# Latent attention: ScalarE copies sums and products out of PSUM, VectorE divides in SBUF in halves, and the marking of choices moves back

## What is computed

```
def attention(x, kv_d_w, q_d_w, k_u_w, v_u_w, q_u_w, rope_k_w, rope_q_w, o_w):
    kv_d, q_d = x @ kv_d_w, x @ q_d_w                     # 512 -> 128
    k, q = ...   # 16 heads of 16 + 16 features, the second 16 rotated (rope)
    v = (kv_d @ v_u_w).reshape(b, s, NH, HD)
    scores = jnp.einsum('bqhd,bkhd->bhqk', q, k) * scale  # causal
    probs = jax.nn.softmax(scores, axis=-1)
    out = jnp.einsum('bhqk,bkhd->bqhd', probs, v).reshape(b, s, H)
    return out @ o_w
h = x + attention(rmsnorm(x, ln1_w), ...)
out = h + moe(rmsnorm(h, ln2_w), ...)     # sigmoid router over 7 experts, the best 2 of each token
```

## Time and profile before

| | |
|---|---|
| time, median of 3 runs | 2374.48 us (2373.86 to 2377.71) |
| profiled execution | 2374.67 us, of it span 2372.9 us |
| TensorE busy | 2136.2 us, 90% of the span |
| VectorE busy | 1362.6 us, 57% |
| ScalarE busy | 805.7 us, 34% |
| GpSimd busy | 669.1 us, 28% |
| granted TensorE clock, mean | 0.96 |
| iterations 0 to 15 of the latent attention | about 1584 to 2041 us; TensorE busy 403.6 of 457 us |

### The profile page before, as it was taken

How to read it: one execution, slowest core, us unless ns; L and a number is a source line. 1 busy time by engine, 2 the same in 40 slices (tenths; PEclk the granted TensorE clock), 3 DMA queues, 4 the chain that set the end, 5 groups by cost and what they waited for, 6 DMA issues and landing times. The chain is left out here.

```text
span 2372.9 us, 31623 instructions
## 1 busy us (share of the span) xinstructions
PE 2136.2 (90%) x10998; PEld 1176.1 (50%) x10999; DVE 1362.6 (57%) x3185; ACT 805.7 (34%) x1333; POOL 669.1 (28%) x945
## 2 busy tenths in 40 slices
PE   9999989989999999879999987588888888889994
PEld 5777748854444444445555543133333333336763
DVE  5866768856222126566777774755656565445443
ACT  5654624420122211334444432523222232123333
POOL 0300014526433321224343443011113131224453
PEclk9999999999999999899999999699999999999997
DMA  7211222270177764363333430200000000065555
GB/s 258 86 36 54 89 104 100 94 292 1 55 235 249 247 190 149 104 130 84 80 88 82 89 68 1 97 3 2 2 19 2 19 28 19 18 184 154 102 98 172
DMA packets 101179, 230.33 MB, mean 97 GB/s; under 512 B 18886, under 2 KB 42626, under 8 KB 93870
## 3 DMA queue, kind: packets, MB, share of 16 engines
q1 hardware_dynamic: 78478, 186.61, 25.5%
q0 software_dynamic: 22560, 41.87, 8.0%
HBM read 169.45 MB, written 63.53 MB: 98 GB/s over the span
## 5 line engine op out<-in xcount | busy, mean ns | idle before, releaser
L2145 DVE CUSTOM_DVE_ANT_0 D_ps<-D_ps,D_mask 128x256 f32<-128x256 f32 (+1 forms) x512 | 186.6, 420 | 60.8 <-PE D_ps L2041 59.9
L1925 ACT ACTIVATE D_probs<-D_ps 128x512 f32<-128x512 f32 (+1 forms) x256 | 125.4, 543 | 178.3 <-PE D_ps L2063 178.2
L1867 POOL TENSOR_SCALAR_AFFINE_SELECT D_probs<-D_probs 128x256 f32<-128x256 f32 x256 | 106.1, 420 | 282.4 <-ACT D_probs L1925 282.3
L3178 DVE TENSOR_REDUCE F_neg_max<-F_ps 128x4 f32<-128x2048 f32 (+1 forms) x64 | 93.9, 1488 | 107.6 <-PE F_ps L3076 101.5
L2928 ACT ACTIVATE F_probs<-F_ps 128x1536 f32<-128x1536 f32 (+1 forms) x48 | 76.4, 1591 | 187.5 <-PE F_ps L3092 187.5
L1400 PE MATMUL C_ps<-C_down_shared,C_hs 128*128 128x512 f32 x256 | 115.4, 600 | 2.4 <-DVE C_hs L1568 2.4
L1388 PE MATMUL C_ps<-C_xT,C_gate_shared 128*128 128x512 f32 x256 | 115.4, 594 | 0.8 <-DMA C_up_shared<-moe_sh_up_dram 0.8
L1388 PE MATMUL C_ps<-C_xT,C_up_shared 128*128 128x512 f32 x256 | 115.1, 592 | 0.0
L2041 PE MATMUL D_ps<-D_k_stack,D_q_stack 96*128 96x256 bf16 (+1 forms) x512 | 93.9, 269 | 15.1 <-DVE D_maxima L2145 12.2
L1237 POOL DMA_INDIRECT expert_sums<-C_y,C_of_slot x32 | 50.3, 1570 | 173.4 <-ACT C_y L1304 111.2
L2809 POOL TENSOR_SCALAR_AFFINE_SELECT F_probs<-F_probs 128x512 f32<-128x512 f32 x64 | 41.1, 654 | 179.9 <-ACT F_probs L2928 179.9
(11 more groups left out here) (578 smaller groups left out, 4943.7 us busy)
## 6 DMA issues: line engine op xcount, KB each, us to landing
C_ring<-moe_experts_dram SPq DMA_DIRECT2D x32, 1536.0 KB, 7.0
qk_parts<-D_parts SPq DMA_DIRECT2D x32, 384.0 KB, 2.6
expert_sums<-A_zeros SPq DMA_DIRECT2D x1, 8192.0 KB
C_ring<-expert_sums SPq DMA_DIRECT2D x5, 1536.0 KB, 13.8
D_q_stack<-qk_parts SPq DMA_DIRECT2D x16, 384.0 KB, 4.7
D_k_stack<-qk_parts SPq DMA_DIRECT2D x16, 384.0 KB, 7.8
B_w<-ctxT_dram SPq DMA_DIRECT2D x1, 4096.0 KB, 16.7
B_c<-ctx_dram SPq DMA_DIRECT2D x4, 1024.0 KB, 7.8
```

Of the source, the lines that this page charges most:

```text
L1867: last = nc.gpsimd.affine_select(now[:, :, 0:P], now[:, :, 0:P], [[0, 2], [1, P]], ALU.is_ge, 0.0, base=0, channel_multiplier=-1)
L1925: nc.scalar.activation(probs[at % 2][:, 2 * pair:2 * pair + 2, 0:w], ps[:, 4 + unit % 3, :].rearrange("p (h q) -> p h q", h=2)[:, :, 0:w], ...
L2145: last = nc.vector.tensor_tensor_reduce(now, now, mask[:, first:256], 1.0, -3e38, ALU.add, ALU.max, maxima[n % 2][:, head, t:t + 1])
L3178: last = nc.vector.tensor_reduce(neg_max[n % 2][:, :, t], ps[:, 0:GROUP, at:at + w], AX_X, ALU.max, negate=True)
```

## The change

ScalarE gets a new step at the head of slot 0, `keep_pv(n)` for the chunk just finished, before the first exponential of the next: it waits for `pv_in_psum`, for the divisions of all chunks before (`oT_ready`), and, from the second batch on, for the output products of the batch before (`out_ready`), and copies bank 5 to `rden` and bank 4 to `oT`. The signal `pv_kept` follows. TensorE's first `times_v` of the next chunk waits for `pv_kept` and no longer for `oT_ready`. VectorE's `divide` waits for `pv_kept` and works in place in SBUF: where the new iteration begins a batch (i % 4 = 0, so also for the last chunk) all 512 columns at slot 0, else 256 columns at slot 0 and 256 at the head of slot 2, where `oT_ready` follows. `mark` of batches 0 to 2 moves from two to four places after "turn_z", to place 3, which is behind the maximum of slot 1; in the last batch it stays where it was.

```diff
--- before.py
+++ after.py
@@ -2727,8 +2727,8 @@
     v_in_psum, v_ready, out_ready, summed = (sem(n) for n in ("v_in_psum", "v_ready", "out_ready", "summed"))
     scores_ready, max_ready, max_turned, m_hi_ready, m_rest_ready, m_mid_ready, m_lo_ready = (sem(n) for n in (
         "scores_ready", "max_ready", "max_turned", "m_hi_ready", "m_rest_ready", "m_mid_ready", "m_lo_ready"))
-    scoresT_ready, exp_ready, cut_ready, probs_read, pv_in_psum, oT_ready = (sem(n) for n in (
-        "scoresT_ready", "exp_ready", "cut_ready", "probs_read", "pv_in_psum", "oT_ready"))
+    scoresT_ready, exp_ready, cut_ready, probs_read, pv_in_psum, pv_kept, oT_ready = (sem(n) for n in (
+        "scoresT_ready", "exp_ready", "cut_ready", "probs_read", "pv_in_psum", "pv_kept", "oT_ready"))
     dve_step = sem("dve_step")
     evicted = {"turn_x": xT_ready, "low": low_ready, "rope": raw_ready, "turn": turned_taken, "nope": nope_ready,
                "values": v_ready, "out": summed, "turn_m": m_rest_ready, "turn_h": h_kept, "logits": zT_ready, "turn_z": e_ready,
@@ -2927,9 +2927,22 @@
                 act.wait_ge(pv_in_psum, n)
             nc.scalar.activation(probs[u][:], ps[:, 0:GROUP, 0:WIDTH[u]], ACT.Exp, scale=1.0 / np.sqrt(HD)).then_inc(exp_ready, 1)
 
+        def keep_pv(n):
+            b, c = divmod(n, GROUP)
+            act.wait_ge(pv_in_psum, n + 1)
+            if n:
+                act.wait_ge(oT_ready, n)
+            if b:
+
+                act.wait_ge(out_ready, GROUP * b)
+            nc.scalar.copy(rden[:], ps[:, 5, :])
+            nc.scalar.copy(oT[:, c, :], ps[:, 4, :]).then_inc(pv_kept, 1)
+
         act.wait_ge(ln1_in, 16)
         for i in range(FIRST, LAST + 1):
             for s in range(SLOTS):
+                if s == 0 and 0 <= i - 1 < CHUNKS:
+                    keep_pv(i - 1)
                 if s % 2 == 0 and 0 <= i < CHUNKS:
                     exponentials(i, s // 2)
                 for at in (2 * s, 2 * s + 1):
@@ -3100,7 +3113,7 @@
                 pe.wait_ge(v_ready, 4 * (b + 1))
                 if n:
 
-                    pe.wait_ge(oT_ready, n)
+                    pe.wait_ge(pv_kept, n)
             for kb, at, w in KEYS[u]:
                 for r in range(GROUP):
                     head = (c * GROUP + r) * HD
@@ -3184,11 +3197,14 @@
             dve.wait_ge(m_mid_ready, n + 1)
             nc.vector.tensor_tensor(m_lo[:], m_rest[:], m_mid[:], ALU.subtract).then_inc(m_lo_ready, 1)
 
-        def keep_oT(n):
-            b, c = divmod(n, GROUP)
-            dve.wait_ge(pv_in_psum, n + 1)
-            steps.after(nc.vector.reciprocal(rden[:], ps[:, 5, :]))
-            nc.vector.tensor_tensor(oT[:, c, :], ps[:, 4, :], rden[:], ALU.mult).then_inc(oT_ready, 1)
+        def divide(n, first, after):
+            c = n % GROUP
+            now = slice(first, after)
+            dve.wait_ge(pv_kept, n + 1)
+            steps.after(nc.vector.reciprocal(rden[:, now], rden[:, now]))
+            last = nc.vector.tensor_tensor(oT[:, c, now], oT[:, c, now], rden[:, now], ALU.mult)
+            if after == S:
+                last.then_inc(oT_ready, 1)
 
         def add(n):
             b, t = divmod(n, 4)
@@ -3296,8 +3312,12 @@
         for i in range(FIRST, LAST + 1):
             for s in range(SLOTS):
                 unit = unit_in(i, s)
-                if s == 0 and 0 <= i - 1 < CHUNKS:
-                    keep_oT(i - 1)
+                if 0 <= i - 1 < CHUNKS:
+                    if i % GROUP == 0:
+                        if s == 0:
+                            divide(i - 1, 0, S)
+                    elif s in (0, 2):
+                        divide(i - 1, s * S // 4, (s + 2) * S // 4)
                 for at in (2 * s, 2 * s + 1):
                     for kind, n in done(i, at, 1, "nope"):
                         join(n)
@@ -3317,9 +3337,12 @@
                     for kind, n in done(i, at, 2, "out", "turn_z"):
                         if kind == "out":
                             normalise_h(n)
+                        elif n < B - 1:
+                            choose(n)
                         else:
-                            if n < B - 1:
-                                choose(n)
+                            mark(n)
+                    for kind, n in done(i, at, 4, "turn_z"):
+                        if n < B - 1:
                             mark(n)
                     for kind, n in done(i, at, 1, "count"):
                         place(n)
```

## The result

The changed kernel takes 2358.80 us (median of 6 runs, 2356.96 to 2365.16), the kernel before beside it 2374.45; the ratio is 0.9936 [0.9921, 0.9951]. The forecast was 2364.0 with a range from 2359.5 to 2371.5: the right side and the right mechanism, and more gain than the range allowed. The profiled execution took 2365.16 us (span 2363.3 us), the longest of its six.

What follows compares the result with a forecast made beforehand. Holes in TensorE's fixed order, waiting for VectorE's maximum, and the clock lost behind them bound the stage. 4.8 + 0.8 + 5.8 - 0.3 - 0.5 = 10.6 us off 2374.67 gave 2364.1, said as 2364; range 2359.5 to 2371.5.

Steps and rivals of the forecast that it cites:

- What bounds the kernel: Latent attention's products: TensorE's work plus holes in its fixed order; 17.0 us waiting for VectorE's maximum, 8.0 in three holes.
- Part 1 and 2: VectorE's half division with gaps 2.3 us where 4.05 stood; ScalarE's copies 1.04 us a pair, charged 0.3 us in all.
- rival (c): Slower: ScalarE's copies delay the exponential by 1.1 us in each of 15 chunks, 2384 us; chance 0.07.
- The three holes: TensorE's waits for the maximum behind the choices shrink by 3.1 to 6.2 us in sum; 4.8 taken.
- rival (a): The port: VectorE loses every such step against GpSimd, holes shrink by only 3.1 us, 2369.4 to 2371 us; chance 0.16.
- The direct waits: Two TensorE waits for the divided output go away, 0.41 us and some 0.4 of 1.16: 0.8 us gained.
- The late rotation: Marking and second half delay the next batch's feature rotation in two chunks: 0 to 1 us lost, 0.5 taken.
- The batch ends: Whole divisions of chunks 3, 7, 11: 0 to 1.3 us late, 0 taken; last chunk 0, ends -0.2 and +1.1.
- The clock: TensorE stays at 2.4 GHz behind the three shrunken holes: 0 to 5.8 us gained, 5.8 taken.
- The sum: Holes 4.8, direct waits 0.8, clock 5.8, less 0.3 for ScalarE and 0.5 for the rotation: 10.6 us gained.
- Rival (d): More than forecast: VectorE wins both races with GpSimd, no rotation is late; 12.5 us gained, 2362 or less; chance 0.10.

Runs made afterwards that it cites:

- before_look3: The kernel before, unchanged, profiled once more; no time of its own is given, its stage is one of the two longest, 526.2 and 526.4 us.
- before_look4: The kernel before, unchanged, profiled once more; no time of its own is given, its first maximum stood at 1564.5 us.

## Why the prediction was right, and where it was wrong

**What bounds the kernel: right.** Holes in TensorE's fixed order were the price, and the three named ones moved the time; the other waits for the maximum are unchanged (0.95, 1.0, 1.24 and 2.4 us in both).

**Part 1 and 2, the prices: right.** A half takes 1.75 us (forecast 1.753), its product 0.42 (0.43), a copy 0.58. The exponential comes 1.43 us behind its first score matmul in iteration 6 (1753.91 - 1752.48), 1.44 before the change (1756.40 - 1754.96): the 0.3 us charged for ScalarE were nothing, and rival (c) fell.

**The three holes: mechanism right, size too small.** Taken were 4.8 us, measured 6.3, just over the upper end of 6.2. The middle was taken between the two outcomes of a race, where the estimate had VectorE ahead by 0.1 us; it was ahead by 0.32 (1756.35 - 1756.03) and won twice. The rule of the Trainium skill that rival (a) names (SBUF — State Buffer, "Who interferes with whom") leaves it to the order in time which of the two waits; so it did not by itself give (a), and with VectorE ahead in two of three races (a) fell. GpSimd's product started where it was forecast, 3.87 us behind the first score matmul (1756.35 - 1752.48; 3.88 before). VectorE's half with its gaps takes 2.13 us (1756.03 - 1753.90) and not 2.3: the next step starts before the row of the product ends. The same 0.2 us is the rest of the gain, 2.47 for 2.25. The direct waits gave 0.41 + 0.36 = 0.8, as forecast: the earlier trace rows end with 1.16 us of waiting, and 0.80 us for GpSimd's cut is left of them.

**The late rotation: 0.5 us charged, 0 paid.** The rotation starts 3.04 us behind the scores (1763.84 - 1760.80), as early as without a choice.

**The batch ends: right for three, wrong for the last.** The products of chunks 3, 7 and 11 take 0.69 us each, so the 0 taken for them held. For the last chunk 0 was taken with a loss of 1.1 as an end; it lost 1.2 us.

**The clock: about right, by two errors.** The three falls are gone, worth by windows of 12 us (1 - 0.74) + 2 x (1 - 0.86) = 0.54, times 12: 6.5 us, for 5.8 forecast. The fall in iteration 13 is new, 1.7 us. Net 4.8. That the stretches stay at 2.4 GHz was argued from one window with 2.5 us of idle in small pieces; the fall in iteration 5 of the same trace, behind waits of 1.53 and 0.82 us, speaks against such a rule and was not looked at.

**The sum.** 6.3 + 0.8 - 1.2 + 4.8 = 10.7 us, where 10.6 was forecast; the stage's length gives 8.9 on average and 9.6 in the four profiles that agree. A part of the difference lies ahead of the change: near 1600 us, before the first changed step, all five profiles of the changed kernel have a stretch of 10.2 us at 1.2 GHz, of the kernel before only before_look3 and before_look4. These two have the longest stages, 526.2 and 526.4 us, and beside them 516.0 is a gain of 10.3. So the sum for the stage held to 2 us, while its terms were off by up to 1.5 with opposite signs; that it held is in part luck.

**The steps that failed.** In the sum it is the term of the three holes: 4.8 us, the middle of an open race, where 6.3 were measured, over even its upper end of 6.2. The last chunk, put at 0, took 1.2 of this back. In the range it is a term put at nothing without a reason: the prediction added ends for the holes and the clock of the stage and none for the rest of the kernel, 1850 us that vary by themselves, and it rested on one profile. Of the 15.6 us between the medians the stage shows 8.9; the start of the stage alone moves by 13.6 us from profile to profile. Where the other 6 to 7 us of the first six runs came from is open. Part of the distance from 2364.0 to 2358.80 was luck of the first six runs: the third timing (2362.34 us, a gain of 10.4) is the forecast. Rival (d), more than forecast, was priced at 2362 or less and given 0.10; with both races won and no rotation late it is the case that happened, though the stage gained 8.9 to 9.6 us and not the 12.5 of (d).

## What to carry to other kernels

When a wait of the bounding engine stands behind two or three steps of another engine, ask which of them the waiting unit doesn't need and move those behind it, before making any of them faster: moving the marking alone gave 9 us of the 11 to 15 by the times and 6.7 of the 8.9 by the stage, and a step that starts later (the whole division behind the copies) took that back. A hole can have a second price in the clock behind it, here 1.7 or 3.4 us; count where the clock falls in the whole stage, since an edit can also move a fall to a hole that it never touched. And before giving a range, look at how much the part that the change doesn't touch varies from run to run.

## What the runs showed of the hardware

- Holes of 2.4 to 3.0 us in TensorE's work behind the three choices cost more than themselves: 12 us behind them ran at 0.72 to 0.86 of the full clock in 23 of 25 cases, 1.7 to 3.4 us each, and at 1.00 behind all 33 holes of up to 1.86 us there. Elsewhere waits of 1.53 and 0.82 us close together had a fall behind them in 18 of 20 profiles in one iteration and in 2 of 20 in another, and the same wait of 2.51 us kept the clock in all six profiles of the kernel before and lost it in all five of the changed one. A hole's size alone doesn't decide; what does is not shown here.
- VectorE beside GpSimd: a step of 0.17 us took 0.61 us behind GpSimd's cut and 1.23 behind its product, and a product of two SBUF operands, 0.69 us alone, took 0.88 when GpSimd's product ended 0.33 us after its start. The Trainium skill states in SBUF — State Buffer, "Who interferes with whom", that such a VectorE instruction and a GpSimd instruction that reads SBUF wait for each other's whole instruction. These rows agree: the short step ends 0.02 and 0.03 us behind GpSimd's instruction, and the product 0.55 us behind it.
- The signal of the last sums reached its reader 1.35 to 1.47 us behind their modelled end in all 20 profiles, whichever engine read it and whether or not matmuls followed. In the other chunks an idle reader mostly started 0.07 to 0.14 us behind it, in some profiles 0.7 us in one or two of them, and once 1.48 us; no run here says why.
